# Rounding the attention probabilities on two engines: one tile of each head on VectorE, the other on GpSimd

## The reference, cut to what matters

```python
sim = jnp.einsum('bhid,bhjd->bhij', _fq(q, dq, 128.0, 8), _fq(k, dk, 128.0, 8)) * SCALE
attn = jax.nn.softmax(sim, axis=-1)
out = jnp.einsum('bhij,bhjd->bhid', _fq(attn, dw, 0.0, 8), _fq(v, dv, 128.0, 8))
```

## Time and profile before

| | before |
|---|---|
| median of the runs, us | 2690.59 (2687.36 to 2694.93) |
| the profiled execution: time, us | 2688.06 |
| the profiled execution: span, us | 2686.3 |
| granted TensorE clock, mean | 0.896 |
| PE / DVE / ACT / POOL busy, us | 2153.1 / 1828.3 / 1131.0 / 939.7 |

### The profile page before, as it was taken

How to read it: one execution, slowest core, us unless ns; L and a number is a source line. 1 busy time by engine, 2 the same in 40 slices (tenths; PEclk the granted TensorE clock), 3 DMA queues, 4 the chain that set the end, 5 groups by cost and what they waited for, 6 DMA issues and landing times.

```text
span 2686.3 us, 42468 instructions
## 1 busy us (share of the span) xinstructions
PE 2153.1 (80%) x10536; PEld 1552.1 (58%) x10536; DVE 1828.3 (68%) x3344; ACT 1131.0 (42%) x1891; POOL 939.7 (35%) x1628
## 2 busy tenths in 40 slices
PE   3489668888878798888978798888879787979786
PEld 2233346665656576665656566665656565657565
DVE  1266667778676867777686867677786868685522
ACT  1222454535454354534454354535444544544211
POOL 1111334334243434344243434343342434342212
PEclk8665889999989899998989899899989898989888
DMA  6765645363535345353535344353535353534010
GB/s 144 229 133 120 120 92 115 79 128 78 129 60 122 75 87 117 79 126 78 128 68 121 71 101 106 79 125 80 122 75 126 66 130 61 119 78 89 27 39 5
DMA packets 750938, 263.78 MB, mean 98 GB/s; under 512 B 661883, under 2 KB 735343, under 8 KB 749999
## 3 DMA queue, kind: packets, MB, share of 16 engines
q1 hardware_dynamic: 747439, 262.13, 45.9%
q10 hardware_dynamic: 3328, 0.01, 0.1%
HBM read 97.01 MB, written 26.60 MB: 46 GB/s over the span
## 4 chain that ended last, share of the span: by engine, by line
PE 45%; DVE 15%; issue 14%; SPq 13%; ACT 5%; DMA 5%; POOL 3%; DVEq 1%; POOLq 0%; ACTq 0%
PE work L1354 18%; PE work L1364 13%; PE outps L1409 5%; PE rowps L1422 4%; SPq L516 4%; DMA PT<-Pn 3%; DVE Pn L1020 2%; ACT E L870 2%; DVE scaled_row L1013 2%; PE work L1625 2%; SPq L507 1%; POOL scs L770 1%; SPq L476 1%; DVE xs L1150 1%; SPq L487 1%
## 5 line engine op out<-in xcount | busy, mean ns | idle before, releaser
L1013 DVE TENSOR_SCALAR_CACHE_REDUCE scaled_row<-rowps,der 128x1024 uint8<-128x1024 f32 x512 | 654.7, 1279 | 340.3 <-PE rowps L1422 339.2
L870 ACT ACTIVATE E<-rowps,ebias,der 128x1024 f32<-128x1024 f32 x512 | 614.9, 1202 | 518.9 <-DVE scaled_row L1013 419.6
L1020 DVE TENSOR_SCALAR Pn<-E,rowinv 128x1024 int16<-128x1024 f32 x512 | 386.3, 755 | 197.0 <-DMA PT<-Pn 157.5
L1422 PE MATMUL rowps<-KC,QM 128*128 128x512 bf16 x1024 | 336.7, 415 | 192.4 <-ACT E L870 184.3
L704 POOL TENSOR_TENSOR rowden<-rowsum,raw 128x1 f32<-128x1 f32 x512 | 116.8, 228 | 1006.8 <-ACT E L870 1006.0
L707 POOL TENSOR_TENSOR rowinv<-rowden,minus 128x1 f32<-128x1 f32 x512 | 337.0, 658 | 92.3 <-POOL rowden L704 92.3
L1409 PE MATMUL outps<-PT,VB 128*16 128x256 f16 x2048 | 294.6, 293 | 0.1
L1354 PE MATMUL work<-hTs,ff_w_sb 128*128 128x256 f32 x1024 | 259.7, 406 | 11.6 <-ACT hTs L846 11.6
L1422 PEld LDWEIGHTS rowps<-KC,QM 128*128 128x128 bf16 x1024 | 88.1, 101 | 300.2 <-ACT E L870 186.7
L1409 PEld LDWEIGHTS outps<-PT,VB 128*16 128x16 f16 x2048 | 173.0, 94 | 132.8 <-issue 85.0
L1354 PEld LDWEIGHTS work<-hTs,ff_w_sb 128*128 128x128 f32 x1024 | 204.3, 203 | 59.7 <-ACT hTs L846 16.5
(11 more groups left out here) (144 smaller groups left out, 3309.4 us busy)
## 6 DMA issues: line engine op xcount, KB each, us to landing
VW<-vw_dram SPq DMA_DIRECT2D x32, 640.0 KB, 4.8
KC<-k_dram SPq DMA_DIRECT2D x64, 256.0 KB, 2.8
K<-k_dram SPq DMA_DIRECT2D x16, 616.0 KB, 3.9
VB<-v_dram SPq DMA_DIRECT2D x64, 128.0 KB, 2.8
PT<-Pn SPq DMA_TRANSPOSE x512, 3.1
V<-v_dram SPq DMA_DIRECT2D x16, 320.0 KB, 3.7
vw_dram<-scs SPq DMA_DIRECT2D x32, 154.0 KB
K<-k_dram SPq DMA_DIRECT2D x16, 308.0 KB, 3.3
```

What stands on the lines that cost most here:

```text
L870: nc.scalar.activation(E[:, slot, :], rowps[n % 2][:], ACT.Exp, bias=ebias[:, n:n + 1], scale=der[:, AL1:AL1 + 1], accum_out=rowsum[:, n:n ...
L1013: nc.vector.tensor_scalar(scaled_row[:, n % 2, :], rowps[n % 2][:], der[:, NAL1:NAL1 + 1], 3.0e38, ALU.mult, ALU.min, accum_out=ebias[:, n ...
L1020: nc.vector.tensor_scalar(Pn[:, n % 2, :], E[:, ring(n)[0], :], rowinv[:, n:n + 1], 255.0, ALU.mult, ALU.min).then_inc(row_round.sem, 1)
L1422: ins = nc.tensor.matmul(rowps[n % 2][:, e * (S // 2):(e + 1) * (S // 2)], QM[:, h % 4, t * P:(t + 1) * P], KC[:, h // 4, e * (S // 2):(e ...
```

## The change

The rounding of odd tiles (e = 1) moves from VectorE to GpSimd; even tiles stay. The one count of rounded tiles, `row_round`, becomes two counts of 16 per unit, and SP, ACT, DVE and POOL wait for the count of the tile's half. On GpSimd the rounding of odd tile n stands in step n, behind `inverse(n)` and the side items due by 2n; on VectorE it had stood in step n+1. GpSimd now carries the waits of an odd rounding, also the one for the transpose of tile n-2.

```diff
-        row_round = count("row_round", ROWT)
+        row_round = [count(f"row_round{t}", H) for t in range(NT)]
...
                 g, e = n // 2, n % 2
-                row_round.wait(sp, v, n + 1)
+                row_round[e].wait(sp, v, g + 1)
...
+            def rounded_probs(n):
+                row_inv.wait(pool, v, n + 1)
+                turned_in[1].wait(pool, v, 16 * (n // 2))
+                nc.gpsimd.tensor_scalar(Pn[:, 1, :], E[:, ring(n)[0], :], rowinv[:, n:n + 1], 255.0, ALU.mult, ALU.min
+                                        ).then_inc(row_round[1].sem, 1)
+
             for n in range(ROWT):
                 if parts["attn"]:
                     inverse(n)
                 beside.until(2 * n)
+                if n % NT == 1 and parts["attn"]:
+                    rounded_probs(n)
                 beside.until(2 * n + 1)
...
                 slot, before = ring(n)
-                row_round.wait(act, v, before + 1)
+                row_round[before % NT].wait(act, v, before // NT + 1)
...
             def rounded_probs(n):
                 row_inv.wait(dve, v, n + 1)
-                turned_in[n % 2].wait(dve, v, 16 * (n // 2))
+                turned_in[0].wait(dve, v, 16 * (n // 2))
                 n = n % ROWT
-                nc.vector.tensor_scalar(Pn[:, n % 2, :], E[:, ring(n)[0], :], rowinv[:, n:n + 1], 255.0, ALU.mult, ALU.min
-                                        ).then_inc(row_round.sem, 1)
+                nc.vector.tensor_scalar(Pn[:, 0, :], E[:, ring(n)[0], :], rowinv[:, n:n + 1], 255.0, ALU.mult, ALU.min
+                                        ).then_inc(row_round[0].sem, 1)
...
             for n in range(ROWT):
-                if tiles(parts, n - 1):
+                if n % NT == 1 and tiles(parts, n - 1):
                     rounded_probs(n - 1)
```

## The result

The changed kernel took 2788.25 us (median of 4 runs, 2781.83 to 2790.86) where the kernel before took 2692.76 (4 runs, 2687.36 to 2696.41) on the same chip: a ratio of 1.0353, with an interval of 1.0327 to 1.0379. It is 95 us slower. The forecast was 2673.6 us, its range ended at 2712, so it was wrong in its sign and in its range.

The account below looks back on a forecast made before the run. Bound by SP's queue in a loop step's first stretch, then VectorE, then TensorE. 25 us less, 15 less and 23 more made 17 less: 2690.6 to 2673.6 us, with an 8-in-10 range of 2635 to 2712.

Parts of the forecast that it names:

- The price of a pass on POOL: One 1024-column rounding on GpSimd: 1.1 us, range 1.05 to 2.35, taken from casts and a two-input pass.
- the dear rounding: Rival, chance 0.15: GpSimd's rounding takes 2.35 us, delaying the store of q and the second subtraction; 2706 us.
- Part 2: Loop step's start: VectorE no longer waits for tile 1's transpose, so SP's stretch begins 1.0 us earlier; 15 us less.
- Part 1: Roundings of tiles 9, 15 and 23 leave VectorE's chain: 1.75 us in 14 loop steps, 25 us less.
- Part 3: Tile 3's rounding on GpSimd delays the casts; SP's store of q waits 1.95 us in 12 loop steps, 23 us more.
- Part 4: Other work behind GpSimd roundings: at 1.1 us tile 9's just fits before the second subtraction; nothing charged.
- The lock rule: Rival, chance 0.15: VectorE and GpSimd lock each other out of shared ports for whole instructions; 47 us more, 2721 us.

Follow-up runs that it names:

- e10: Changed kernel with only the roundings of tiles 9 and 11 of each unit on GpSimd, all others on VectorE: 2779.6 us, ratio 1.0335 to the kernel before.
- e9: Changed kernel with only the roundings of tiles 1 and 3 of each unit on GpSimd, all others on VectorE: 2731.0 us, ratio 1.0149 to the kernel before.
- e2: Changed kernel with GpSimd's odd roundings cut to 256 of 1024 columns, the rest left out: 2650.0 us, ratio 0.9856 to the kernel before.
- e4: Kernel before with VectorE's odd roundings cut to 16 of 1024 columns, nothing moved to GpSimd: 2647.1 us, ratio 0.9857.
- e8: Changed kernel with only the roundings of tiles 13, 15 and 23 on GpSimd, all others on VectorE: 2637.2 us, ratio 0.9811 to the kernel before.
- e11: Changed kernel with only the roundings of tiles 17, 19 and 21 on GpSimd, all others on VectorE: 2686.5 us, ratio 0.9997 to the kernel before.
- e1: The probe: kernel before plus a tail timing forms of a GpSimd pass alone, then roundings beside VectorE's; the full rounding alone took 3.70 us.

## Why the prediction was wrong

**The price of a pass on POOL** is the term that was mis-sized. I took 1.1 us with bounds of 1.05 and 2.35; it is 3.71. The casts were the wrong neighbour: a real cast of this shape takes 1.04, as the slope from the earlier trace rows had it (1.05), but a multiply by a per-row value is another form. The upper bound rested on the thought that a pass with two tensor inputs must be dearer than one with one. The probe shows the reverse: 1.89 against 2.84 for the same product. No row of before bore on this form over many columns, so the range had no right to end at 2.35. With the right price the prediction's own working gives 2741 us, so this term alone leaves 47 us of the 2788 unexplained. The second step that failed is the list of what stands behind a rounding on POOL, told under the rival and Parts 2 to 4.

**The rival that came true** was the dear rounding, with its threshold: it said 1.75 us, and the lengths tried cross the kernel before near 1.8. That is luck: the gain at a short pass was 38 us, not 17, and the slope just above it 65 us for a us, not 26, and the two errors cancel. Its working, with the right price, gives 2673.6 + 2.6 x 26 = 2741 us, not 2788: its slope was 26 us for a us and the runs show 54. It charged two places, the store of q and L770. It missed r11 ahead of the cast `q2T` (2.6 us on the chain in 10 units of e10, 26 us), r31 ahead of the exponent of tile 1 (Part 2 below), and ACT, which waits for the cast behind r3 as SP does (58.8 us in all; 66.9 in e9). What ACT's wait costs no run isolates: e2 has 51.0 us of it and is faster than the kernel before.

**Part 1** had the right mechanism and half its size. Without the odd roundings on DVE the kernel is 38 us shorter (e4), and with only r13, r15 and r23 on POOL 51 (e8); I had 25. I counted only pieces of one step's chain. The chain's share of the rounding falls from 2.4% to 1.5% of the span in e8, 64 to 40 us, so 24 of the 51 us are the pieces themselves. The other 27 I can't place with certainty, and as the profiled executions of e8 and e4 do not differ and the two intervals touch, 38 and 51 may be one gain. I had charged r23 with half its gain for the meeting with L802; e8 doesn't separate it.

**Part 2** did not come. SP's wait for xs stayed (21.5 us in 13 waits). DVE is rid of r1, but the residual is no earlier: it comes 22.4 us behind the step's store of the output (1366.92), where it came 21.5 behind it (1311.68). Another odd rounding holds it now, r31 of the unit before. Pieces of the chain of the changed kernel (start us, us, what):

```profile
1353.83 3.71 POOL Pn L714
...
1359.76 4.96 PE work L1373 x16
...
1366.92 0.70 DVE xs L1159
```

The exponent of tile 1 waits for r31, PE's scores for the exponent, and the residual's product stands behind the scores. r31 is on the chain with its whole 3.7 us in 12 of the 16 units. Part 4 had called r31 on POOL a gain that SP's order hides. No run moved tile 31 alone, so its price is open; it is among the 16 us left above. Nor did Part 2's gain come with r31 left on DVE: in e9 SP's wait for xs is 10.8 us, 4 less than before.

**Part 3** was right in mechanism and, with the right price, in the size of the wait: (1.95 + 2.6) x 12 = 55 us, and SP's wait for the casts is 75.4 us in e9 and 77.1 in the change, 21.7 before: 54 and 55 more. That e9, which has r1 and r3 alone on POOL, is just the 55 - 15 = 40 us longer is partly luck: the 15 are Part 2's, of which e9 shows 4. That r1 and r3 were tried together leaves the share of each open.

**Part 4** said that r9 just fits ahead of L770 at 1.1 us and costs all that it takes beyond. At 3.71 that is 2.6 us a step, and in e10 the whole 3.71 stands on the chain. r17 and r19 were called harmless, and e11 shows it (2686.5 us, 0.9997). r11 wasn't looked at, and r5 was tried in no run of its own.

**The lock rule** (the Trainium skill, SBUF — State Buffer, section "SBUF: two separate sides") was weighed at 47 us. The row: L1029's mean is 967 ns, where it was 755, and its median 754. Where the stretches lie: between 400 and 2400 us, even roundings that began while POOL was in a rounding took 0.91 us in the mean (11 of them), those that began in a pass with two tensor inputs, L746, 1.60 us (13), and with POOL idle 0.75 (47). By that rule the odd rounding, POOL's longest pass, should have been the worst to meet; the measurement decides, and it held VectorE up little, while the passes with two inputs did. 256 x 0.21 = 54 us of DVE time were lost in all, a fifth of the 282 that the rival reckoned; by its own 17% that is 9 us on the chain. One such meeting in the timeline of the changed kernel, even rounding beside L746:

```profile
1390.97 1.27 POOL L746 TENSOR_TENSOR xs<-xs,rows 128x512 f32<-128x512 f32 x1
1391.13 1.66 DVE L1029 TENSOR_SCALAR Pn<-E,rowinv 128x1024 int16<-128x1024 f32 x1
```

**PE's clock** was in no step. Ten us from about the rounding r3 on (at 1318.46 before, at 1374.11 after), first of the kernel before, then of the changed one, last the same place of a step of e2 (from:to, length, PE busy, granted clock, DMA share, GB/s):

```profile
1320.16:1330.16 10.00, 9.03 (x45) 1.00 0.92 213
```
```profile
1374.52:1384.52 10.00, 6.59 (x28) 0.76 0.37 97
```
```profile
1306.99:1316.99 10.00, 6.59 (x17) 0.66 0.60 154
```

Behind r3, PE was busy for 9.03 of 10 us at full clock (2.4 GHz), and is busy for 6.59 at 0.76, part of it at the lower level of 1.2 GHz. So there is a gap in PE's work and a lower clock around it, and in the thirteen steps PE's busy time is up by 32 us of the 74. But e2 has the same gap and the same dip in this place and is 38 us faster than the kernel before, and e9 is 40 us slower at a mean clock of 0.896, that of the kernel before; the change has 0.873 and e10 0.875. So this dip does not make the loss, and what the lower clock adds to it no run isolates.

**What would show it**, as the prediction listed: 256 instructions on each engine, yes; 193 us on DVE, no (247.6); about 1.1 us on POOL, no; "the prediction is wrong if POOL's rounding holds the next step's inverse so long that ACT waits for it": the inverse is held, and it is DVE that waits for it (260.5 us), while ACT waits for the rounding itself (166.1).

## What to carry to other kernels

Before work is handed to another engine, find a row of the same instruction form there, and where there is none, let the range be as wide as not knowing: on POOL a cast and a multiply by a row's value differ by a factor of 2.7, with the cap 3.6. What is put into an in-order queue is priced by what stands behind it, tile by tile: the same 3.7 us pass gained 17 us a place over three places and cost 45 a place over two, in the mean. Moving only three tiles for which little waits (e8, where ACT's exponents wait 9.3 us for them in all) gave 1.9% where moving all lost 3.5%.

## What the runs showed of the hardware

- A POOL tensor_scalar over 1024 f32 columns takes 3.70 us with two steps, 2.84 with one, 3.62 with a factor given in the instruction, 3.70 with an f32 output, and 1.99 for 512 columns; a cast of that shape takes 1.04, a product with two tensor inputs 1.89 (e1). The Trainium skill (GPSIMD Engine Reference, section "Engine selection") calls passes with one input roughly line-rate; the cast, not far above the 0.755 us of VectorE's rounding of that shape, fits that, the tensor_scalar, at nearly five times this, doesn't.
- Such a pass lets VectorE work beside it, but each hinders the other: beside two of them five of VectorE's eight roundings took 0.75 to 0.77 us and three 1.40 to 1.48, and the two passes took 4.63 and 4.44 us, against 3.70 alone (e1).
- Two steps with the same work differed by 3.3 us of 148 with the granted clock at 0.95 and 0.92, in one and the same execution (e8).
